# Start of the feed-forward stage, and the planner's weights, in a cross-attention and feed-forward layer

## The reference, cut to what matters

```python
x = x + xattn(layernorm(x), pos, ctx, ...)     # first stage: rat_read, attention, rat_write, small mlp, rat_write
xn = layernorm(x)                              # second stage: feed-forward
def binary(w, base):                           # w, base: 3 pairs of (3584, 1024) fp32
    d = w - base
    return base + mean(abs(d)) * sign(d)       # the mean goes over the whole matrix
h = silu(xn @ binary(w1, m1).T) * (xn @ binary(w3, m3).T)
x = x + h @ binary(w2, m2).T
```

## Time and profile before

| | us |
|---|---|
| three runs, median (lowest to highest) | 1540.93 (1533.27 to 1541.52) |
| the profiled execution, device time | 1538.53 |
| its span in the trace | 1536.6 |

### The profile page before, as it was taken

One profiled execution on the slowest core, in us unless ns is written; L12 is line 12 of the kernel. 1 busy time (PEld: TensorE's weight loads), 2 busy tenths in 40 slices (PEclk: granted clock), 3 DMA queues, 4 the chain that ended last, 5 costly groups with the idle time before them and its releaser, 6 DMA issues.

```text
span 1536.6 us, 17442 instructions
## 1 busy us (share of the span) xinstructions
PE 1327.6 (86%) x6622; PEld 1043.3 (68%) x6622; DVE 876.5 (57%) x1172; ACT 547.5 (36%) x990; POOL 563.4 (37%) x350
## 2 busy tenths in 40 slices
PE   4877778777776706999999999999999999999999
PEld 3855444445554505888888888888888888888887
DVE  7646656547778564355554655646365554645543
ACT  4555655665554315222223222222222222222220
POOL 3654666658666355122222221212122212121210
PEclk8788888788786856999999999999999999999999
DMA  8466666575545222222232323232322232222212
GB/s 329 148 219 218 226 214 215 184 224 191 163 147 161 72 96 80 86 85 107 83 110 82 110 82 110 83 110 83 110 83 98 94 108 84 107 86 90 102 55 110
DMA packets 78022, 197.61 MB, mean 129 GB/s; under 512 B 9314, under 2 KB 9588, under 8 KB 77428
## 3 DMA queue, kind: packets, MB, share of 16 engines
q1 hardware_dynamic: 77940, 196.50, 37.3%
HBM read 192.27 MB, written 4.19 MB: 128 GB/s over the span
## 4 chain that ended last, share of the span: by engine, by line
PE 66%; DVE 14%; DMA 6%; issue 6%; ACT 4%; POOL 3%; SPq 1%; DVEq 0%; ACTq 0%; POOLq 0%
PE pair L884 40%; PE quad L898 16%; DMA part_base<-in_mean_w 5%; POOL part_w L1494 2%; PE pair L850 1%; DVE wr_a L1269 1%; ACT part_w L1073 1%; PE pair L642 1%; DVE yn L1162 1%; DVE wr_a L1265 1%; PE quad L850 1%; PE pair L770 1%; DVE negwide L1217 1%; PE quad L733 1%; DVE raw_w L1370 1%
## 5 line engine op out<-in xcount | busy, mean ns | idle before, releaser
L1509 POOL TENSOR_TENSOR raw_w<-raw_w,raw_base 128x1024 f32<-128x1024 f32 x84 | 215.2, 2561 | 685.9 <-DMA raw_base<-in_mean_w 685.9
L884 PE MATMUL pair<-xnT_hi,w_hi 128*128 128x512 f32 x896 | 349.8, 390 | 0.0
L884 PE MATMUL pair<-xnT_hi,w_lo 128*128 128x512 f32 x896 | 349.5, 390 | 0.0
L884 PE MATMUL pair<-xnT_lo,w_hi 128*128 128x512 f32 x896 | 349.5, 390 | 0.0
L1494 POOL TENSOR_TENSOR part_w<-part_w,part_base 128x512 f32<-128x512 f32 x168 | 229.1, 1368 | 165.4 <-DMA part_base<-in_mean_w 164.2
L1420 DVE TENSOR_TENSOR hf<-sgf,pair 128x512 f32<-128x512 f32 x56 | 38.5, 688 | 296.1 <-PE pair L884 296.1
L1095 ACT ACTIVATE w_hi<-raw_w 128x1024 fp32r<-128x1024 f32 x84 | 88.9, 1058 | 325.7 <-DVE raw_w L1370 325.7
L884 PEld LDWEIGHTS pair<-xnT_hi,w_lo 128*128 128x128 f32 x896 | 168.7, 188 | 35.1
L884 PEld LDWEIGHTS pair<-xnT_lo,w_hi 128*128 128x128 f32 x896 | 168.6, 188 | 35.0
L884 PEld LDWEIGHTS pair<-xnT_hi,w_hi 128*128 128x128 f32 x896 | 168.7, 188 | 34.7
L898 PE MATMUL quad<-w_hi,h_hi 128*128 128x512 f32 x448 | 175.4, 392 | 9.2 <-DVE hid L1393 9.2
(11 more groups left out here) (235 smaller groups left out, 1592.1 us busy)
## 6 DMA issues: line engine op xcount, KB each, us to landing
part_w<-in_w SPq DMA_DIRECT2D x168, 256.0 KB, 3.0
part_base<-in_mean_w SPq DMA_DIRECT2D x168, 256.0 KB, 4.1
raw_w<-in_w SPq DMA_DIRECT2D x84, 512.0 KB, 3.7
raw_base<-in_mean_w SPq DMA_DIRECT2D x84, 512.0 KB, 4.6
qk_xa<-in_x SPq DMA_DIRECT2D x8, 512.0 KB, 3.8
out<-work SPq DMA_DIRECT2D x8, 512.0 KB, 2.6
inner<-in_x SPq DMA_DIRECT2D x4, 512.0 KB, 8.8
ctxw<-in_ctx SPq DMA_DIRECT2D x1, 2048.0 KB, 19.5
```

The source lines that it names most:

```text
L884: a = pe.matmul(pair[:, b, :], ww[:, k, :], xx[:, k, b * SEQ:(b + 1) * SEQ], start=k == 0 and n == 0, stop=k == KF - 1 and n == 2)
L1509: pool.tensor_tensor(w[:, :], w[:, :], base[:, :], ALU.subtract).then_inc(f_diff, 1)
```

## The change

1. **Memory.** The tensors of the first stage are allocated in zones: first those that are dead when attention is over (`big`, `vaug`, `probs`, `oT`, `wqkv`, `yn`, `yT` and others), then those that die with the measuring and the mlp (`parts`, `ctxw`, `inT`), then `xT`, then the rest. Over the first zone lie the `xnT` of batch 0, the 3 raw buffers, the 3 buffers of `w13` and `work0`; over the second the `xnT` of batch 1; over `xT` `work1`. The second stage's w2, h and gate buffers lie behind.
2. **New nodes in the first stage's order**: "raw" (load, difference and sign of the first 3 weights), "coef" (the coefficients), "prep" (whole weight, upper and lower half of these 3), "norm" (the normalised rows of all 8 tiles, all on ACT now, two `work` buffers), "early" (the products of the first 3 weights with batch 0, in banks 4, 6 and 0, 4 nodes of 6 matmuls each). They are taken out of the second stage.
3. **The second stage** begins on PE with the products of these 3 weights with batch 1 (banks 5, 7, 1), then goes on as before from the fourth weight. SP, POOL and ACT go on with the fourth weight at once after their order; `phase_one_over` loses its wait for `me_abs` and is no longer waited for by SP and POOL.
4. **Planner**: many assumed durations in `WORK` are set anew (most of them longer, on DVE above all), `PULL` goes from 0.001 to 0.00768, `MEASURE_WEIGHT` from 2.2 to 1.993, and each stage gets an offset on its rank (`FIRST`).

```diff
 RAT = ...
-       ("ACT", 0.85), ("POOL", 2.2), ("POOL", 1.8), ("DVE", 3.9)]
+       ("ACT", 0.85), ("POOL", 2.3), ("POOL", 2.0), ("DVE", 4.7)]
...
+    "raw": [("SP", 2.0), ("POOL", 2.5), ("ACT", 1.05)],
+    "coef": [("DVE", 0.6), ("PE", 0.3), ("DVE", 0.25)],
+    "prep": [("DVE", 1.6), ("ACT", 1.05), ("DVE", 1.5)],
+    "norm": [("ACT", 1.25), ("PE", 1.6), ("ACT", 1.05), ("DVE", 1.25)],
+    "early": [("PE", 1.4)] * 4,
...
+EARLY_BANK = (4, 6, 0)
+EARLY = len(EARLY_BANK)
...
+    elif stage == "raw":
+        if part == 0:
+            after("weigh", T_UNIT[-1], 0)
+            after("row", TILES - 1, 0)
+    elif stage == "coef":
+        if part == 0:
+            after("measure", UNITS - 1, 2)
+    elif stage == "prep":
+        if part == 0:
+            after("raw", t, 2)
+            after("coef", 0, 2)
+    elif stage == "norm":
+        if part == 0:
+            after("finish", t, 16)
+            after("norm", t - 2, 1)
+            ...
+            elif t == 1:
+                after("back", TILES - 1, 14)
+        elif part == 2 and t == TPB:
+            after("mlp", BATCH * HALVES * MT - 1, 0)
+            after("measure", UNITS - 1, 2)
+    elif stage == "early":
+        if part == 0:
+            after("prep", t, 2)
+            after("norm", TPB - 1, 3)
...
-            rank = start - PULL * weight[key]
+            rank = start - PULL * weight[key] - FIRST.get(stage, 0.0)
...
-MEASURE_WEIGHT, PULL = 2.2, 0.001
+MEASURE_WEIGHT, PULL = 1.993, 0.00768
+FIRST = {"mlp": 0.3, "fq": -1.6, "raw": -0.9, "weigh": -0.7, "x": 0.5, "prep": -0.2, "coef": 0.5, "early": -1.1, "row": 0.7,
+         "out": -0.3, "fc": -0.1, "diag": -0.6}
...
+        def attention_over(eng):
+            eng.wait_ge(at_pv, len(T_UNIT))
+            eng.wait_ge(rw_t, TILES)
...
+                elif stage == "raw":            # SP
+                    attention_over(sp)
+                    load_raw(t)
+            for n in range(EARLY, len(NEED)):
+                sp.wait_ge(f_lo, n - RAWS + 1)
+                load_raw(n)
...
+                elif stage == "early":          # PE
+                    if part == 0:
+                        pe.wait_ge(f_lo, t + 1)
+                        pe.wait_ge(n_lo, TPB)
+                        banks_free(pe, "early", t, 0)
+                    gate(t, 0, range(2 * part, 2 * part + 2))
             for g in range(JT // GROUP):
+                if g == 0:
+                    pe.wait_ge(n_lo, TILES)
+                    for u in range(EARLY):
+                        readers_through(pe, [had_last[gate_bank(u, 1)]])
+                        gate(u, 1, range(KF))
+                for s in range(EARLY if g == 0 else 0, 4):
...
+                elif stage == "coef":           # DVE
+                    if part == 0:
+                        ...
+                        dve.wait_ge(me_abs, UNITS)
+                        dve.tensor_reduce(csum[:, :], absum[:, :, :], AX.X, ALU.add).then_inc(c_sum, 1)
```

More of the change, by code:

```diff
@@ L300, in choose @@
         stage, t, part = key
-        if key == ("fill", 0, 0):
+        if stage == "early" and part == 0:
+            choices = [(EARLY_BANK[t],)]
+        elif key == ("fill", 0, 0):
             choices = [tuple(range(ATTENTION_BANKS))]
@@ L508, in banks_free, with readers_through @@
         def banks_free(eng, *key):
-            for stage, t, part in had[key]:
+            readers_through(eng, had[key])
+        def readers_through(eng, users):
+            for stage, t, part in users:
                 if stage == "fq":
@@ L780, in rat_out, with passes, gate @@
                               ).then_inc(ro_low[n], 1)
+            def passes(stat, mov):
+                return [(stat[0], mov[0]), (stat[1], mov[0]), (stat[0], mov[1])]
+            def gate(u, b, ks):
+                for k in ks:
+                    for n, (ww, xx) in enumerate(passes(w13[u % W13], xnT[b])):
+                        a = pe.matmul(banks[gate_bank(u, b)], ww[:, k, :], xx[:, k, :],
+                                      start=k == 0 and n == 0, stop=k == KF - 1 and n == 2)
+                if k == KF - 1:
+                    a.then_inc(g_mm, 1)
             pe.wait_ge(ld_const, 80)
@@ L870, in passes @@
-            def passes(stat, mov):
-                return [(stat[0], mov[0]), (stat[1], mov[0]), (stat[0], mov[1])]
-            for g in range(JT // GROUP):
-                for s in range(4):
+                elif stage == "coef":
+                    pe.wait_ge(c_ones, 1)
+                    pe.wait_ge(c_sum, 1)
+                    banks_free(pe, "coef", 0, 1)
+                    pe.matmul(bank_of("coef", 0, 1)[:, 0:3], ones, csum[:, :], start=True, stop=True).then_inc(c_mm, 1)
+                elif stage == "norm":
+                    pe.wait_ge(n_wk, t + 1)
+                    banks_free(pe, "norm", t, 1)
+                    turn_blocks(lambda k: works[t % 2][:, k * P:(k + 1) * P], KF, banks2_of("norm", t, 1)).then_inc(n_t, 1)
+                elif stage == "early":
+                    if part == 0:
[3 more added lines that the diff above has]
+                    gate(t, 0, range(2 * part, 2 * part + 2))
@@ L879, in _ @@
                     for b in range(BATCH):
[L880 to L886 removed]
+                        gate(u, b, range(KF))
@@ L1068, in _ @@
                         rsqrt(st[:, 13:14], 1, st[:, 14:16], (fi_var, t + 1), fi_rstd)
+                elif stage == "raw":
+                    sign(t)
+                elif stage == "prep":
+                    upper(t)
+                elif stage == "norm":
+                    norm(t, part)
                 elif stage == "measure":
```

316 lines of the change are left out of this document (154 added, 162 removed).

## The result

The changed kernel takes 1474.57 us (median of 4 runs, 1471.71 to 1485.18) against 1539.05 us for the kernel before (4 runs): ratio 0.960, 95% interval 0.954 to 0.966. The forecast was 1479 us and 0.96. The profiled execution took 1476.49 us with a span of 1474.6 us, 62.0 us less than before.

The account below looks back on a forecast made before the run. PE was taken to bound the kernel: a dense matmul stream after a 41.2 us hole. Hole -34.4, moved products -16.3 and T -9 (order -15, added work +6) sum to -59.7 from 1538.5: 1479 us, range 1455 to 1505.

Parts of the forecast that it names:

- The hole: PE mostly idle between the last tile's statistics (563.49) and the first product (604.69), 41.2 us; forecast 34.4 us less.
- T: End of the last tile's statistics on DVE, at 563.49 before; forecast to move by -9 us.
- Products moved out of the stream: 72 matmuls, three weights by batch 0, leave PE's dense stream for the idle stretch before it: 16.3 us less.
- The doubt about the clock: PE's clock might be at half speed for the moved products, costing up to 16.5 us; 0 was taken.
- The fourth weight: Its preparation was expected to be covered by 10.9 us of PE work on second and third weight; nothing charged.
- Added work in front of T: Rows, weights and coefficients add 16.7 us of DVE work; 6 us charged on T, bounds 0 and 16.7.
- The contention rule: VectorE instructions with two SBUF inputs and GpSimd instructions reading SBUF block each other; six weight instructions priced at 8.6 us.
- The order: The planner's new numbers rearrange the whole first stage, 563 us; -15 us taken, bounds from +25 to -77.
- The sum: -34.4 - 16.3 - 9 = -59.7 against the profiled execution's 1538.5 us, so 1479 us, 0.96 of before.
- (c): Added work or its waits replace the hole, or early products run past T: about 1508 us, chance 0.17.
- (d): Measuring is pushed back and DVE stands waiting for the coefficients; typical price 1550 us, chance 0.04.
- (e): Early products and weights are placed at the very end of the order; gain about 18 us, 1520, chance 0.03.

Follow-up runs that it names:

- diff_late: Changed kernel, but POOL's differences of the fourth and later weights wait for the last tile's statistics: 1467.9 us, ratio 0.953.
- no_early: Changed kernel, but the 72 products of the first three weights with batch 0 are made after the last tile's rows: 1488.2 us, ratio 0.968.
- rows_late: Changed kernel, but no tile's normalised rows are made before the last tile's statistics, weights and coefficients staying early: 1512.8 us, ratio 0.984.
- weights_late: Changed kernel, but the first three weights' nodes and the early products moved to the end of every engine's order: 1487.5 us, ratio 0.968.
- old_planner: Changed kernel's structure with the planner's old durations, pull 0.001, measuring weight 2.2 and no offsets: 1510.5 us, ratio 0.983.
- new_durations: Changed kernel with the planner's new durations but the old pull and measuring weight and no offsets: 1529.5 us, ratio 0.994.

## Why the prediction was right, step by step

**The hole.** 34.4 us forecast, 33.2 measured: T + 8.0 for T + 6.8. The step held, with one detail wrong. I charged the 1.2 us to the one pair of banks left, and those were free at 553.89, when tile 6's lower half was done, 0.1 us after tile 7's rows were ready (553.76). What held tile 7's turn until 555.99 was the third weight's second half of products on PE, made at the low clock. In the changed kernel's second execution the turn isn't held and the hole is 4.8, less than the 5.6 of the trip in the forecast, because the turn takes 1.09 us where the forecast's took 1.97. One reading behind the step was loose: the 10.14 us that POOL waited for its first difference began before T; 6.3 of them lie behind it.

**Products moved out of the stream.** 16.3 us forecast, 16.7 measured. The 1.4 us of low clock at the stream's start, which I left in, went too in both executions of the changed kernel: the first 24 products take 5.56 and 5.58 us, where they took 7.06 before. The forecast had no term for this, and diff_late (7.08) shows that it isn't sure to come. Some 1.1 us came back further down the stream; where was not looked into. The 18.6 us of no_early are the same 16.3 and a start at the low clock. The doubt about the clock was fair for a part of the moved products: the third weight's first product takes 0.79 us after 9.29 us of idleness, while the first weight's, behind other PE work, takes 0.50. The clock is 0.59 of full from 541 to 546 and 0.57 from 551.2 to 556, where the third weight's two halves lie. But the first 48 products were through in 11.2 us, at a clock of 1.00. By the rule of the Trainium skill (TensorE: Matmul & The Clock Gate, What's actually happening) the clock follows how busy TensorE has been, and the trace agrees for both parts. What I had got wrong was the case: two thirds of the products stood behind other PE work and not in an idle stretch. The price of 16.5 us didn't come.

**The fourth weight.** Its products start at 575.85, straight behind the third's, and its lower half had been done since 567.97. The cover held.

**Added work in front of T.** 6 us forecast between 0 and 16.7. T - M grew by 8.7 (38.4 to 47.1), by 6.6 in the second execution, and by 9 to 11 under the planner's other numbers. rows_late and weights_late have 4.6 and 5.5 us less of it (2.5 and 3.4 against the second execution), which says no more than that rows and weights both count. The size was right within 3 us, the reason partly: I had put the rows and weights into DVE's idle time between 500 and 540, and most of it is there, but in the profiled execution half of the 8.7 us (two steps of 2.3 us for 0.16) is the wait for POOL's differences, of which I had only counted the three of the early weights. The fourth's and fifth's, which the change lets start before T, are the ones that hurt. The third slow step, beside the sum into `hid`, isn't new: before has it too, 2.16 us at 557.49.

**The contention rule.** From the Trainium skill (SBUF — State Buffer, Who interferes with whom) I had priced six waits of weights at 8.6 us. That pricing was wrong: the lower halves that run between 513 and 541 take 1.17 to 1.22 us and the whole weights 1.28, no wait at all. The row that I set beside it, a product of 128x768 at 2.97 us "against a mean below 1", was misread too: the sixteen of that line before take 0.96 to 2.97 us, with a median of 1.90, and 0.96 is the shortest. The rule itself holds: a VectorE instruction with two SBUF inputs waits out the POOL instruction beside it, whatever its own size, so that it cost 2.1 us on instructions of 0.16 here.

**The order.** -15 us forecast between -77 and +25, M moved by -20.8. The coefficients, which I had put at 510 to 530, were there at 504.66 with it. This was the term with the least behind it, and the runs show why: the same nodes give an M of 504, 537 or 560 under three sets of numbers. It came out right by a choice within bounds, not by a reading. The argument with the DMA waits on the chain isn't supported either: after, the chain still spends 5% of its span on them, as before, and 8% in the second execution, the shorter one.

```profile
PE pair L864 40%; PE quad L982 16%; DMA part_base<-in_mean_w 5%; POOL part_w L1595 3%; PE pair L846 2%; PE quad L846 1%; DVE raw_w L1369 1%; DVE wr_a L1360 1%; ACT part_w L1201 1%; DVE negwide L1308 1%; PE pair L737 1%; DVE wr_a L1345 1%; ACT prob L1047 1%; PE quad L809 1%; DVE yn L1253 1%
```

**The sum.** The order came out 5.8 us better than forecast, the added work 2.7 worse, the hole 1.2 worse and the moved products 0.4 better; the total is 2.3 us off because these partly cancel, so a part of that closeness is luck.

**The rivals.** (c), the added work in place of the hole, was real at 8.7 us and is what old_planner and new_durations grew into: with numbers that let new nodes pass the mlp's last multiplies, among what else they change, the same structure gives 0.983 and 0.994. (d) didn't come up: the measuring ended on POOL at 502.7, before the old 513.8, and the coefficients were there at 504.66. (e) didn't come up either. weights_late, which puts these nodes at the end of every engine's order, is that case: 1487.5 us where I had priced it at 1520, since the rows made early keep the start at T + 10.4 and the order's gain stays.

## What to carry to other kernels

A stretch in which PE idles between two stages is best priced as three terms: how long after the last input the first product could come if nothing were queued ahead of it, how much product work fits into the idle stretch in front, and how much the added preparation lengthens the last inputs' own chain. The first two were read from the trace to about 2 us here. The third is a question of order: the new nodes under the old weights of the planner gave 26 of the 62 us, so compare times at a mark in front of the new work (M) and behind it (T) before blaming the new work. Filling the idle stretch had a second use: a turn of rows with products right in front of it took 1.0 to 1.1 us, and 1.97 behind an idle PE. When one stage's loads are let start earlier, look at what their first consumer shares with the critical engine.

## What the runs showed of the hardware that I had not expected

A DVE step on a single column per partition, 0.16 us alone, took up to 2.32 us beside a POOL instruction of 2.4 us, three times in one chain; with two of those three POOL instructions moved away the two steps took 0.16 again. A chain of such small steps can lose many times its own length beside POOL. A step with one input, 128x48, which takes 0.18 us at its shortest, took 1.83 beside a POOL addition of 128x768 (525.26 in the trace after). M varied by up to 6.5 us between executions with the same order up to it, more than several of the effects sought; the cause wasn't looked for.
